# A decoder's gated-decay attention: the token stage by batch instead of by blocks of four tiles, softplus by products of sigmoids, row sums on TensorE

## What is computed

```python
q = (x @ W_q.T).reshape(Bx, Sx, H, DH)
k = (x @ W_k.T).reshape(Bx, Sx, H, DH)
v = x @ W_v.T
b = (q * k).sum(-1) * SCALE
alpha = (x @ W_alpha_w.T + W_alpha_b).reshape(Bx, Sx, H, DH)
a = -jax.nn.softplus(alpha).sum(-1)
vs = jnp.sign(v)
...
vl = jnp.log(jnp.abs(v) + EPS)
...
def step(carry, inp):
    ln, nm, sg = carry
    a_t, b_t, vl_t, vs_t = inp
    ln = _stable_lse(a_t + ln, b_t)
    dec = a_t[..., None] + nm
    new = b_t[..., None] + vl_t[:, None, :]
    m = jnp.maximum(dec, new)
    ssum = sg * jnp.exp(dec - m) + vs_t[:, None, :] * jnp.exp(new - m)
    nsg = jnp.sign(ssum)
    nsg = jnp.where(nsg == 0, jnp.ones_like(nsg), nsg)
    nm = m + jnp.log(jnp.abs(ssum) + EPS)
    y = (nsg * jnp.exp(nm - ln[..., None])).sum(-2)
    return ((ln, nm, nsg), y)
...
return y @ W_o.T
```

## Time and profile before

| | |
|---|---|
| median of 3 runs | 1100.84 us (1100.56 to 1105.02) |
| profiled execution | 1104.72 us, its span 1103.0 us |
| busy in the span | TensorE 950.9 (86%), VectorE 766.2 (69%), ScalarE 584.3 (53%), GpSimd 446.0 (40%) |
| granted TensorE clock | 0.9 of full |
| chain that ended last | PE 41%, POOL 19%, issue 17%, DVE 14%, ACT 4%, DMA 3% |

### The profile page before, as it was taken

How to read it: one execution, slowest core, us unless ns; L and a number is a source line. 1 busy time by engine, 2 the same in 40 slices (tenths; PEclk the granted TensorE clock), 3 DMA queues, 4 the chain that set the end, 5 groups by cost and what they waited for, 6 DMA issues and landing times.

```text
span 1103.0 us, 17860 instructions
## 1 busy us (share of the span) xinstructions
PE 950.9 (86%) x5321; PEld 797.5 (72%) x5321; DVE 766.2 (69%) x1989; ACT 584.3 (53%) x1361; POOL 446.0 (40%) x488
## 2 busy tenths in 40 slices
PE   6999999999986999990776478887959999999994
PEld 5899999999974568770554478776737888888883
DVE  4666666666668643430468899945858989999985
ACT  3666666666656533440576444434635555555554
POOL 3566665656563214637873366642440000000001
PEclk8999999999998698995788688885969999999998
DMA  6223232323214101342210567101007566566641
GB/s 241 76 96 101 85 102 84 101 85 101 97 54 150 39 10 46 87 73 31 31 17 1 83 84 74 31 1 34 24 19 196 158 179 179 164 172 175 175 143 38
DMA packets 57456, 100.36 MB, mean 91 GB/s; under 512 B 7217, under 2 KB 34545, under 8 KB 57154
## 3 DMA queue, kind: packets, MB, share of 16 engines
q1 hardware_dynamic: 51362, 94.74, 31.3%
q0 software_dynamic: 6048, 5.05, 3.2%
HBM read 77.35 MB, written 22.41 MB: 90 GB/s over the span
## 4 chain that ended last, share of the span: by engine, by line
PE 41%; POOL 19%; issue 17%; DVE 14%; ACT 4%; DMA 3%; SPq 1%; POOLq 0%; DVEq 0%; ACTq 0%
PE PS L1666 8%; PE PS L1667 8%; PE PS L1668 8%; POOL P L631 7%; POOL Xp L713 4%; POOL WS L640 3%; PE PS L1862 3%; DVE r0b L1480 2%; POOL WS L636 2%; DVE rb L1493 2%; PE PS L1876 2%; ACT Xp L434 1%; PE PS L1811 1%; PE PS L1817 1%; DMA Wb<-decay 1%
## 5 line engine op out<-in xcount | busy, mean ns | idle before, releaser
L631 POOL TENSOR_TENSOR P<-P,rl 128x256 f32<-128x256 f32 (+1 forms) x130 | 104.8, 827 | 122.0 <-DVE rl L1146 122.0
L427 POOL TENSOR_TENSOR rs<-ms,neghalf 128x4 f32<-128x4 f32 x24 | 26.2, 1091 | 312.9 <-DVE nm L421 312.8
L1064 ACT ACTIVATE FG<-PS 128x512 f32<-128x512 f32 x120 | 71.8, 598 | 111.1 <-PE PS L1668 111.1
L1139 DVE CUSTOM_DVE_ANT_0 P<-PS,cmask 128x128 f32<-128x128 f32 (+1 forms) x260 | 77.1, 352 | 70.6 <-issue 70.5
L857 ACT ACTIVATE P<-P,mn 128x128 f32<-128x128 f32 (+1 forms) x260 | 114.3, 444 | 1.9 <-DVE mn L1139 1.9
L1666 PE MATMUL PS<-XTh,W 128*128 128x512 f32 x256 | 101.7, 397 | 0.4
L1667 PE MATMUL PS<-XTl,W 128*128 128x512 f32 x256 | 101.1, 395 | 0.0
L1668 PE MATMUL PS<-XTh,W 128*128 128x512 f32 x256 | 101.1, 395 | 0.0
L1737 PE MATMUL PS<-VO,PT 128*128 128x128 f32 x804 | 100.6, 275 | 0.0
L1652 DVE TENSOR_TENSOR FU<-FG,PS 128x512 f32<-128x512 f32 x120 | 82.6, 688 | 25.2 <-PE PS L1668 25.2
L1737 PEld LDWEIGHTS PS<-VO,PT 128*128 128x128 f32 x804 | 95.0, 192 | 0.0
(11 more groups left out here) (426 smaller groups left out, 2644.2 us busy)
## 6 DMA issues: line engine op xcount, KB each, us to landing
GI<-coef SPq DMA_DIRECT2D x60, 256.0 KB, 4.0
GW<-coef SPq DMA_DIRECT2D x60, 256.0 KB, 4.1
w3s<-WS SPq DMA_DIRECT2D x32, 384.0 KB, 2.6
W<-w3s SPq DMA_DIRECT2D x32, 384.0 KB, 3.2
Wb<-decay SPq DMA_DIRECT2D x7, 1024.0 KB, 14.8
WR<-in_w SPq DMA_DIRECT2D x32, 192.0 KB, 2.5
WR<-in_w SPq DMA_DIRECT2D x16, 256.0 KB, 2.8
w12f<-WS SPq DMA_DIRECT2D x16, 256.0 KB, 2.1
```

What stands on the lines that cost most here:

```text
L631: last = pool.tensor_tensor(v, v, f, ALU.mult)
L1064: act.activation(FG[:, k % 2, :], bank(4 + k % 2), ACT.Silu).then_inc(sem("fg_done"), 1)
L1139: dve.tensor_tensor_reduce(out=P[:, slot, c:c + w], in0=scores(par, q), in1=cmask[:, 256 - w:256], scale=1.0, scalar=3e38, op0=ALU.add, op ...
```

## The change

- **Rows back.** POOL gathers both routed rows of a batch (two tiles) plainly into GA and GB, four transfers a batch, without a wait for their landing. TensorE adds X, GA and GB with three f32 products by the identity into bank b % 2 (`pair_sum`); batch 0 alone is added by VectorE. Statistics and norm read that bank. The norm, the split and `values` go by batch: transposes in bank 5, then the values in the same bank, then the next batch's transposes, with one token product between.
- **Softplus.** softplus(z) = max(z, 0) - ln sigmoid(|z|): ScalarE takes |z|, relu, copies q, and a sigmoid; VectorE multiplies 32 sigmoids at a time with one reduce (PROD), and one reduce of 1,024 elements sums q·k and relu together. A single Ln over the products serves four batches. GpSimd's adds, ZR and `softplus_sums` go. q has one bank (4) where it had two.
- **Decays.** In two halves of four batches (32 rows of 256 tokens each): the first half inside the token loop (logs in batch 4, levels in batch 5, weights in batch 6, low half in batch 7), the second inside the first three rounds of the state stage. SP writes each half when it is ready. Four selectors are made once, before the tokens; the context products move ahead of the tokens too.
- **PSUM and SBUF** are laid out anew for that; the last tile's products stand behind the first weights of batch 0.

The sums of the batch after next stand between a tile's products and the transposes of the next batch; before, none stood there. The diff, cut:

```diff
+        wu = [sb(f"wu{q}", [32, 2, S], F32, sd) for q in range(2)]
+        WUr = [sb(f"WUr{q}", [64, 2, S], F32R, sd) for q in range(2)]
+        dsel = [sb(f"dsel{k}", [64, H1, 128], F32R, sd) for k in range(4)]
...
+        GA = sb("GA", [128, T, 128], F32, sd1)
+        GB = sb("GB", [128, T, 128], F32, sd1)
...
+        XT2, QB = bank(5, S), bank(4)
...
+            def decay_out(q):
+                sp.wait_ge(sem("wu_ready"), q + 1)
+                sp.dma_start(decay[q * 32:q * 32 + 32, :], wu[q][:, 0, :]).then_inc(sem("decay_out"), 16)
+                sp.wait_ge(sem("decay_out"), on("decay_out", 16 * q + 16))
...
+            decay_out(0)
             for g in range(1, B):
+                if g == 4:
+                    decay_out(1)
...
-            def rows_back(s, c):
-                for t in tiles(c):
-                    pool.indirect_dma_start(out=X[:, t, :], out_offset=None, in_=yrows, compute_op=ALU.add,
-                                            in_offset=bass.IndirectOffsetOnAxis(ap=pidx[:, s, t:t + 1], axis=0)).then_inc(sem(f"y{'ab'[s]}_in{c}"), 16)
+            def rows_back(b):
+                for s, y in enumerate((GA, GB)):
+                    for t in pair(b):
+                        pool.indirect_dma_start(out=y[:, t, :], out_offset=None, in_=yrows,
+                                                in_offset=bass.IndirectOffsetOnAxis(ap=pidx[:, s, t:t + 1], axis=0)).then_inc(sem(f"ya_in{b % 4}"), 16)
...
-            for c in range(NC_):
-                rows_back(0, c)
-                if c:
-                    ln_factors(pool, 2, c - 1)
...
-            for t in range(T):
-                pool.wait_ge(sem("z_ln"), t + 1)
-                pool.wait_ge(sem("z_pos"), t + 1)
-                pool.tensor_tensor(ZR[:, t, :], ZR[:, t, :], ZA[:, t, :], ALU.add).then_inc(sem("z_sp"), 1)
...
+            rows_back(0)
+            for b in range(1, B):
+                rows_back(b)
+                if b == 2:
+                    pool.memset(mb[:, 0:1], -BIG).then_inc(sem("d_init"), 1)
+                    pool.memset(db[:, 0:1], 0.0).then_inc(sem("d_init"), 1)
+                ln_factors(pool, 2, b - 1)
+            ln_factors(pool, 2, B - 1)
...
+            act.wait_ge(sem("sel32_done"), 1)
+            for b in range(4):
+                act.activation(dsel[b][:, :, :], sel32[:, 8 * b:8 * b + 8].rearrange("p (h o) -> p h o", o=1).to_broadcast([64, H1, 128]),
                                ACT.Copy).then_inc(sem("dsel_done"), 1)
...
+            def pair_norm(b):
+                act.wait_ge(sem("ln_factor"), 2 * turn(2, b) + 2)
+                for t in pair(b):
+                    act.activation(X[:, t, :], part(sum2(b), t) if b else X[:, t, :], ACT.Identity, scale=rs[:, t:t + 1], bias=nb[:, t:t + 1]).then_inc(sem("ln_x"), 1)
...
+            def query_and_decay(t):
+                p = t % 2
+                act.wait_ge(sem("dz_ready"), t + 1)
+                if t >= 2:
+                    act.wait_ge(sem("z_prod"), t - 1)
+                act.activation(ZA[:, p, :], bank(6 + p), ACT.Abs).then_inc(sem("z_abs"), 1)
+                if t >= 2:
+                    act.wait_ge(sem("b_sum"), t - 1)
+                act.activation(PRZ[:, p, 1, :], bank(6 + p), ACT.Relu).then_inc(sem("z_pos"), 1)
+                act.wait_ge(sem("dq_ready"), t + 1)
+                act.activation(QS[:, p, :], QB, ACT.Copy, scale=1.0 / math.sqrt(64)).then_inc(sem("qs_done"), 1)
+                act.wait_ge(sem("z_abs"), t + 1)
+                act.activation(ZA[:, p, :], ZA[:, p, :], ACT.Sigmoid).then_inc(sem("z_sig"), 1)
...
+            def log_products(q):
+                act.wait_ge(sem("z_prod"), 8 * q + 8)
+                act.activation(LNP[:, q, :], PROD[:, q, :, :, :, :].rearrange("p r s b h -> p (r s b h)"), ACT.Ln).then_inc(sem("z_ln"), 1)
...
+            for b in range(1, B):
+                query_and_decay(2 * b)
+                if b + 1 < B:
+                    pair_hi(b + 1)
+                if b == 4:
+                    log_products(0)
+                if b == 5:
+                    decay_in(0, bank(0))
+                if b == 6:
+                    decay_exp(0)
+                if b == 7:
+                    first_weights(0)
+                query_and_decay(2 * b + 1)
+                if b + 2 < B:
+                    pair_norm(b + 2)
+                if b == 6:
+                    decay_high(0)
+            first_weights(1)
...
+                if g == 1:
+                    decay_exp(1)
+                if g == 2:
+                    decay_high(1)
...
+                    dve.wait_ge(sem("y_sum"), b)
+                else:
+                    x = X[:, 0:2, :]
+                    dve.wait_ge(sem("ya_in0"), on("ya_in0", 64))
+                    dve.tensor_tensor(x, x, GA[:, 0:2, :], ALU.add).then_inc(sem("first_sum"), 1)
+                    dve.wait_ge(sem("first_sum"), 1)
+                    dve.tensor_tensor(x, x, GB[:, 0:2, :], ALU.add).then_inc(sem("first_sum"), 1)
...
+            def products_and_sums(t):
                 p = t % 2
-                if t % 4 == 0 and t < T - 4:
-                    combined_stats(t // 4 + 1)
+                dve.wait_ge(sem("z_sig"), t + 1)
+                dve.tensor_reduce(PROD[:, t // 8, t % 2, :, t % 8 // 2, :], ZA[:, p, :].rearrange("p (h s d) -> p s h d", h=H1, s=2), AX.X, ALU.mult).then_inc(sem("z_prod"), 1)
                 dve.wait_ge(sem("qs_done"), t + 1)
                 dve.wait_ge(sem("dk_ready"), t + 1)
-                dve.tensor_tensor(PR[:, p, :], bank(2 + p), QS[:, p, :], ALU.mult).then_inc(sem("pr_done"), 1)
-                dve.wait_ge(sem("z_abs"), t + 1)
-                dve.tensor_scalar(ZR[:, t, :], bank(6 + p), 0.0, None, ALU.max).then_inc(sem("z_pos"), 1)
+                dve.tensor_tensor(PRZ[:, p, 0, :], bank(2 + p), QS[:, p, :], ALU.mult).then_inc(sem("pr_done"), 1)
+                dve.wait_ge(sem("z_pos"), t + 1)
                 dve.wait_ge(sem("pr_done"), t + 1)
-                dve.tensor_reduce(ABs[:, 1, t, :], PR[:, p, :].rearrange("p (h d) -> p h d", h=H1), AX.X, ALU.add).then_inc(sem("b_sum"), 1)
-                if t % 4 == 2 and t < T - 4:
-                    ln_lo(dve, 2, t // 4 + 1)
...
-            for t in range(4, T, 2):
-                softplus_sums(t, t + 2)
...
+            def decay_low(q):
+                dve.wait_ge(sem("wu_hi"), q + 1)
+                dve.tensor_tensor(WUr[q][32:64, :, :], wu[q][:, :, :], WUr[q][0:32, :, :].bitcast(F32), ALU.subtract).then_inc(sem("wu_done"), 1)
+
...
+            pair_stats(2)
+            pair_lo(1)
+            products_and_sums(1)
+            signed_values(1)
+            for b in range(1, B):
+                if b == 7:
+                    decay_low(0)
+                products_and_sums(2 * b)
+                if b + 1 < B:
+                    pair_lo(b + 1)
+                if b + 2 < B:
+                    pair_stats(b + 2)
+                if b == 4:
+                    log_decays(0)
+                if b == 6:
+                    decay_weights(0)
+                products_and_sums(2 * b + 1)
+                if b == 5:
+                    decay_levels(0)
+                if b + 1 < B:
+                    signed_values(b + 1)
...
+                if g == 0:
+                    log_decays(1)
+                if g == 1:
+                    decay_levels(1)
...
+                if g == 1:
+                    decay_weights(1)
+                if g == 2:
+                    decay_low(1)
...
+            def pair_sum(b):
+                pe.wait_ge(sem(f"ya_in{b % 4}"), on(f"ya_in{b % 4}", b // 4 * 64 + 64))
+                pe.wait_ge(sem("shared_added"), on("shared_added", NC_))
+                if b >= 3:
+                    pe.wait_ge(sem("ln_x"), T * 2 + 2 * b - 2)
+                for n, y in enumerate((X, GA, GB)):
+                    last = pe.matmul(sum2(b), ident[:, :], y[:, 2 * b:2 * b + 2, :].rearrange("p t d -> p (t d)"), start=n == 0, stop=n == 2)
...
+            def pair_T(b):
+                if b:
+                    pe.wait_ge(sem("vp_done"), 2 * b)
...
+                    last = pe.transpose(part(XT2, t), X[:, t, :], ident[:, :])
...
+            def values(b):
+                bb, w = slice(b * S, b * S + S), slice(3 * CH, 3 * CH + 128)
+                pe.wait_ge(sem("ln_lo"), NC_ + b + 1)
+                mm3(XT2, (wdh[:, w], wdl[:, w]), (XTh[:, bb], XTl[:, bb])).then_inc(sem("dv_ready"), 1)
...
+            def token_products(t):
+                p, tok_cols = t % 2, slice(t * 128, t * 128 + 128)
+                for n, dst, what, free, lag in ((2, bank(6 + p), "dz_ready", "z_pos", 2), (0, QB, "dq_ready", "qs_done", 1), (1, bank(2 + p), "dk_ready", "pr_done", 2)):
+                    if t >= lag:
+                        pe.wait_ge(sem(free), t - lag + 1)
+                    w = slice(n * CH, n * CH + CH)
+                    if n == 2:
```

(36 more changed lines are left out.)

304 lines of the change are left out of this document (139 added, 165 removed).

## The result

The changed kernel takes **1092.74 us** in the median of six runs (1089.18 to 1094.26), the one before 1100.7 (1099.48 to 1105.86) on the same chip: a ratio of 0.9918, 95% interval 0.9896 to 0.9940. By the ratio that is 9.0 us less (6.6 to 11.4 by the interval); the two medians by themselves differ by 8.0. The forecast was 1082 us, 18.8 less. The sign is right and the time lies in the range, but over half of the expected gain didn't come.

What follows compares the result with a forecast made beforehand. No engine bound the token stage; engines waited for one another, then came a serial VectorE tail. Start 532.0, tokens to 589.7, states to 717.9 against 736.9: 19.0 us less, 1085.7 from the profile, 1082 as median; range 1070 to 1096.

Steps and rivals of the forecast that it cites:

- Start: From first gathers at 498.85: first product at 512.2 instead of 527.53, VectorE's steady token work from 532.0.
- Steady tokens: Token loop: VectorE bounds at 6.95 us a batch; 52.0 us plus 5.7 of bubbles, leaving the tokens at 589.7.
- through bank 5: Token loop: TensorE, ScalarE and VectorE tied through bank 5's transposes and values; 0.3 us a batch, 1.8 in all.
- Tail and first round: Between tokens and states: last sums, scans, decay write and 13.66 us transfer leave the path; first round 9.2 us.
- States: State stage: 113.1 us after the first round, plus 5.9 for the second half's decays on VectorE; end at 717.9.
- Gathers at 1.54: Token gathers: plain yrows gathers cost POOL as much as adding ones, so POOL bounds; 1091 us, chance 0.12.
- A reduce at the scan's rate: Token loop: VectorE's product reduce takes 0.76 us more for each of 16 tiles; 1094 us, chance 0.07.
- TensorE the bound at its lower level: Token loop: TensorE's clock drops, 12.4 us a batch; slower, 1113 us, chance 0.09.
- Loads that block for double: ScalarE's table loads each block it for about double their row, 6 us; 1088 us, chance 0.04.
- A pipe that doesn't overlap: Token loop: three near-equal engines alternate, 1.5 us more a batch, 10 us; 1092 us, chance 0.10.
- Batch 4 late: State stage: second half's decays come late and batch 4 waits for its transfer, up to 14 us; 1096 us, chance 0.03.
- rival 2: Token loop: VectorE's product reduce runs like its scan, 12 us more in all; 1094 us, chance 0.07.

Runs made afterwards that it cites:

- the run with thin floors: Against the changed kernel, GpSimd's floors in rounds 0 to 2 of the state stage compute one column in place of 1020; one execution took 1086.32 us.

## Why the prediction was half right

**Start: right.** Gathers at 0.94 and 1.25 apart, first product 13.37 us after the first gather against 13.35; VectorE's steady work 33.66 after it against 33.15. The factors were cheaper (1.02 us for two tiles against 1.36), but norm and transposes behind them took as much longer, and filling the pipe lost 0.5 us.

**Steady tokens: right but for a size.** From 529.92 to 588.92 is 59.0 us; forecast 57.7. The multiplying reduce runs at the adding one's 0.60 us from start to start, not at the scan's rate, and the extra 1.3 us is small change: 2.53 a tile for 2.46, 0.9 for the signed values with their wait. The bubbles came to 5.6 us against 5.7, but by luck:

- Forecast 0.3 a batch "through bank 5". It was 0.54 to 0.64, only ahead of batches 2 to 4 (the 0.53 ahead of batch 1 belongs to the start), and another ring: ScalarE takes the norm of batch b+2 and then four steps of the next tile, the sigmoid last. The run with the sigmoid sooner shows it.
- The Ln pair cost 1.11, not 2.1. One of its two loads ran beside VectorE's work; the Exp pair cost nothing, as said.
- Batch 7 cost 2.69, not 1.8. TensorE is at its lower level there (0.63 us a matmul against 0.39), which the term left out.

**Tail and first round: right.** The sums, the decay scans, the reciprocal and the 13.66 us transfer are off the path, and round 0 took 9.54 us for 9.2.

**States: the step that failed** is "scans, reciprocal and low half of batches 4 to 7, 1.9 + 3.4 + 0.65 = 5.9, on the engine with no gaps, so paid". The work was priced by durations from a stretch where GpSimd was idle, and put into one where it is busy 39.8 of 55.1 us. Where it was put it held VectorE 12.0 us (605.10 to 608.92, 615.90 to 622.65, 636.38 to 637.85), against 5.8 for the same steps in the token loop: 6.2 of standing still behind GpSimd's instructions. Another 0.5 us are waits for TensorE (0.26 in round 1, 0.17 at the end) that disappeared with the floors, which makes the 6.7 of the run with thin floors. With the same instructions ahead of the floors the states took 128.26 us against the forecast's 128.2. The other 1.5 us is the end wait, which the forecast took over from the kernel before and whose cause stays open. Together 8.2 of the 8.4 us by which the states overran; the tokens overran by 1.8; that is the 10.2.

The prediction looked for this in the wrong place: "GpSimd's floors keep their slack" asks only whether GpSimd would be late. It named no rival in which the two engines hold each other up. The Trainium skill has it (SBUF — State Buffer, section SBUF: two separate sides): VectorE and GpSimd share a pair of interfaces to SBUF, a VectorE instruction with two SBUF inputs contends for it with a GpSimd instruction that reads SBUF, and whichever starts first keeps it for its whole instruction. By that rule each of the second half's two-operand steps could wait up to a floor instruction. The traces here agree in both directions: VectorE's line 1498 went from 0.41 to 2.38 us, and the floor that GpSimd began at 616.97, when line 1505 had not ended (617.54), took 2.73 in place of 2.34.

**The rivals.** Gathers at 1.54: no, 0.94. A reduce at the scan's rate: no. TensorE the bound at its lower level: no, granted 1.00 from 530 to 554 and PE busy 7.5 of 8 us, so not far from it. Loads that block for double: no, the one in batch 4 runs 553.51 to 554.79 and the Ln starts at 554.81; nothing stands between them. A pipe that doesn't overlap, 1.5 us a batch: no, 0.6. It would have given 1092, the time measured, for a reason that didn't act. Batch 4 late: no, even with copies of 13.9 us. The prediction's own sums have slips that change nothing: 20 matmuls at 0.23 are 4.6 and not 4.7, the steps of the first round add to 9.1 and not 9.2, and its chances give 0.81 for faster without rival 2, so that 0.83 holds little of that rival and not most.
